# Text context enters with its features on the partitions; keys are multiplied one round sooner

## The reference

```python
# cross attention, 16 heads of 16
q  = layernorm(x) @ Wq + bq
kv = ctx @ Wkv + bkv                      # keys and values of each head
attn = softmax(q . k / 4) over the 77 rows
x1 = x + (attn @ v) @ Wp + bp
# mixture of experts: 8 experts, hidden 1024, the best 2 of each token
xf = layernorm(layernorm(x1)) * g + b
gate = softmax of the two highest of xf @ router_w
expert_e(t) = clip(clip((t_n @ W1 + b1) * silu(clip(t_n @ W2 + b2))) @ Wo + bo)
out = x1 + sum over the two experts of gate_e * expert_e(xf)
```

## Time and profile before

| | before |
|---|---|
| median of 3 runs | 937.87 us |
| lowest, highest | 937.62, 942.07 us |
| span of the profiled execution | 940.2 us (its own run time is not listed apart) |
| instructions | 19225 |
| PE busy | 897.5 us (95%) |
| DVE busy | 745.6 us (79%) |
| ACT busy | 648.5 us (69%) |
| POOL busy | 410.9 us (44%) |
| attention rounds, first scores to first expert product | 19.5 to 309.3 us |

### The profile page before, as it was taken

How to read it: one execution, slowest core, us unless ns; L and a number is a source line. 1 busy time by engine, 2 the same in 40 slices (tenths; PEclk the granted TensorE clock), 3 DMA queues, 4 the chain that set the end, 5 groups by cost and what they waited for, 6 DMA issues and landing times.

```text
span 940.2 us, 19225 instructions
## 1 busy us (share of the span) xinstructions
PE 897.5 (95%) x6206; PEld 806.6 (86%) x6206; DVE 745.6 (79%) x1757; ACT 648.5 (69%) x1305; POOL 410.9 (44%) x649
## 2 busy tenths in 40 slices
PE   5999999999999988999999999999999999999995
PEld 3788887887888877888999989899898998998994
DVE  2678888788688888887988888787877877878893
ACT  3666766767558774776877776776766777767773
POOL 3555576777567577322433150504204233043052
PEclk9999999999799999999999999999999999999998
DMA  5332233342246217744656545736817828566442
GB/s 141 62 66 56 65 87 75 79 99 68 49 111 202 101 65 281 220 121 129 175 135 171 168 119 196 226 119 169 267 66 192 308 54 247 201 163 175 162 79 26
DMA packets 132625, 129.18 MB, mean 137 GB/s; under 512 B 59984, under 2 KB 117408, under 8 KB 132384
## 3 DMA queue, kind: packets, MB, share of 16 engines
q1 hardware_dynamic: 119648, 110.36, 38.5%
q0 software_dynamic: 12864, 17.44, 10.3%
HBM read 102.01 MB, written 25.36 MB: 135 GB/s over the span
## 4 chain that ended last, share of the span: by engine, by line
PE 81%; DVE 7%; issue 4%; ACT 4%; POOL 1%; another core or an unknown queue 1%; SPq 1%; DMA 0%; POOLq 0%; DVEq 0%; ACTq 0%
PE bank L2002 36%; PE bank L2046 19%; PE bank L1835 5%; PE bank L1755 3%; PE bank L1994 3%; PE bank L1812 3%; PE bank L1773 3%; PE bank L1971 2%; PE bank L2034 1%; PE bank L1802 1%; DVE maxes L1256 1%; PE bank L1858 1%; PE bank L1820 1%; DVE probs L1262 1%; PE bank L1868 1%
## 5 line engine op out<-in xcount | busy, mean ns | idle before, releaser
L860 POOL DMA_INDIRECT out_rows<-yo,token x68 | 114.1, 1678 | 379.3 <-ACT yo L1111 314.6
L2002 PE MATMUL bank<-xh,wh 128*128 128x512 f32 (+1 forms) x672 | 234.7, 349 | 2.0 <-DVE gate_in L1628 1.4
L2002 PE MATMUL bank<-xl,wh 128*128 128x512 f32 (+1 forms) x672 | 229.1, 341 | 0.0
L2002 PE MATMUL bank<-xh,wl 128*128 128x512 f32 (+1 forms) x672 | 228.4, 340 | 0.0
L1604 DVE TENSOR_TENSOR wl<-raw,wh 128x1024 fp32r<-128x1024 f32 x126 | 152.6, 1222 | 12.8 <-ACT wh L1042 11.0
L2046 PE MATMUL bank<-wh,hh 128*128 128x256 f32 x496 | 142.1, 286 | 1.1 <-issue 1.0
L2046 PE MATMUL bank<-wl,hh 128*128 128x256 f32 x496 | 140.7, 284 | 1.0 <-issue 1.0
L2002 PEld LDWEIGHTS bank<-xh,wh 128*128 128x128 f32 x672 | 128.3, 191 | 15.5 <-DVE gate_in L1628 2.8
L2046 PE MATMUL bank<-wh,hl 128*128 128x256 f32 x496 | 140.8, 284 | 0.0
L2002 PEld LDWEIGHTS bank<-xh,wl 128*128 128x128 f32 x672 | 128.0, 190 | 14.9
L2002 PEld LDWEIGHTS bank<-xl,wh 128*128 128x128 f32 x672 | 128.4, 191 | 10.9
(11 more groups left out here) (198 smaller groups left out, 1882.0 us busy)
## 6 DMA issues: line engine op xcount, KB each, us to landing
raw<-in_W SPq DMA_DIRECT2D x42, 1024.0 KB
raw<-in_Wo SPq DMA_DIRECT2D x25, 1024.0 KB
whole<-in_W SPq DMA_DIRECT2D x8, 1024.0 KB, 6.6
xs<-in_x SPq DMA_DIRECT2D x32, 128.0 KB, 2.6
out_rows<-x SPq DMA_DIRECT2D x32, 128.0 KB, 1.8
shared<-z_rows SPq DMA_DIRECT2D x7, 520.0 KB
bo_row<-in_bo SPq DMA_DIRECT2D x25, 128.0 KB
k_blocks<-k_parts SPq DMA_DIRECT2D x128, 19.2 KB
```

The costliest lines, as they stand in the source:

```text
L860: e.indirect_dma_start(out=out, out_offset=bass.IndirectOffsetOnAxis(ap=token[j % 4][:, s:s + 1], axis=0), in_=yo[j % 2][:, s, :], in_offs ...
L2002: mm = e.matmul(ps[:, h * cols:(h + 1) * cols], ws[split_before(j) % 2][:, w, c, m * P:(m + 1) * P], xx[j % 2][:, c, 0:cols], start=(h == ...
```

## The change

The host hands the context over as `[8 pairs, 128 features, 2 chunks, 2 batches, 77 rows]`, so one DMA of 128 partitions fills the tile `c_t` that PE reads; there are now two such tiles. `transpose_ctx` on PE and `ctx_t` on ACT are gone. `keys_of_pair`, `keys` and `low_keys` move one round sooner, to the rounds -3, 1, 5, ... 25. SP loads `wk` and `wv` with a counter each, and ahead of `wq`; it stores the values of batch 0 between the first four and the last four pieces of its keys; and it issues the key pieces of odd batches one round sooner, in the rounds -1, 3, 7, .... The turns of the two shared banks shift with the removed use.

```diff
-def ctx_pair(i):
+def key_pair(i):
     return (i + 3) // 4 if (i + 3) % 4 == 0 and 0 <= (i + 3) // 4 < BATCH // 2 else None
...
-        uses += [("k", nb // 2)] if batch and even and nb % 2 == 0 else []
+        uses += [("k", key_pair(i))] if key_pair(i) is not None else []
...
-        uses += [("ctx", ctx_pair(i))] if ctx_pair(i) is not None else []
...
-        cs = [raw[2][0:CTX, 1, i * D:(i + 1) * D] for i in range(2)]
-        c_t, k_t = (raw[2][:, 0, i * 2 * DC * CTX:(i + 1) * 2 * DC * CTX].rearrange(
-            "p (c s k) -> p c s k", c=DC, s=2) for i in range(2))
+        *c_t, k_t = (raw[2][:, 0, i * 2 * DC * CTX:(i + 1) * 2 * DC * CTX].rearrange(
+            "p (c s k) -> p c s k", c=DC, s=2) for i in range(3))
...
-            def load_ctx(b):
-                if b >= 2:
-                    e.wait_ge(ctx_t_mm, b // 2)
-                e.dma_start(cs[b % 2][:, :], a["ctx"][b * CTX:(b + 1) * CTX, :]).then_inc(
-                    f_ctx[b % 2], 16)
+            def load_ctx(t):
+                if t >= 2:
+                    e.wait_ge(v_mm, 2 * (t - 1))
+                e.dma_start(c_t[t % 2][:, :, :, :], a["ctx"][t]).then_inc(f_ctx[t % 2], 16)
...
             load_ctx(0)
             e.dma_start(qk_bias[:, :], a["qk_bias"]).then_inc(f_const, 16)
-            load_ctx(1)
+            load_weights(f_wk, wk, "wk")
             load_x(1)
-            load_weights(f_kv, wk, "wk")
+            load_weights(f_wv, wv, "wv")
             load_weights(f_wq, wq, "wq")
+            load_row(f_bv, 0, "bv")
             load_x(2)
-            load_weights(f_kv, wv, "wv")
-            load_row(f_bv, 0, "bv")
...
                 load_rest(i)
+                if (i + 7) % 4 == 0 and 2 <= (i + 7) // 4 < BATCH // 2:
+                    load_ctx((i + 7) // 4)
                 if batch and i % 2:
                     load_values(nb)
-                    if nb % 2 == 0 and nb + 2 < BATCH:
-                        load_ctx(nb + 2)
-                        load_ctx(nb + 3)
...
                     store_x1(i - 2)
+                if i % 2 and 0 <= nb + 1 < BATCH and (nb + 1) % 2:
+                    spread_keys(nb + 1)
                 if batch and i % 2 == 0:
                     if nb == 0:
-                        spread_keys(nb)
+                        spread_keys(nb, range(HPB))
                     store_values(nb)
-                    if nb:
+                    if nb == 0:
+                        spread_keys(nb, range(HPB, HPC))
+                    elif nb % 2 == 0:
                         spread_keys(nb)
...
-            def ctx_t(t):
-                e.wait_ge(ctx_t_mm, t + 1)
-                if t:
-                    e.wait_ge(v_mm, 2 * t)
-                e.activation(c_t[:, :, :, :].rearrange("p c s k -> p (c s k)"),
-                             misc_of("ctx", t)[:, 0:2 * DC * CTX], ACTF.Copy).then_inc(
-                                 ctx_t_out, 1)
...
-                if batch and even and nb % 2 == 0:
-                    keys(nb // 2)
+                if key_pair(i) is not None:
+                    keys(key_pair(i))
...
+                if key_pair(i) is not None:
+                    low_keys(key_pair(i))
                 if batch and not even:
                     low_queries(nb)
...
-                if 0 < nb < BATCH and even and nb % 2 == 0:
-                    low_keys(nb // 2)
...
-                if batch and even and nb % 2 == 0:
-                    keys_of_pair(nb // 2)
+                if key_pair(i) is not None:
+                    keys_of_pair(key_pair(i))
...
-                if ctx_pair(i) is not None:
-                    transpose_ctx(ctx_pair(i))
```

More of the change, by code:

```diff
@@ L275, in build @@
         v_flat = nc.dram_tensor("v_flat", [BATCH, KEYS, VW], F32, kind="Internal").ap()
-        f_const, f_bv, f_rows, f_kv, f_wq, f_wp, f_router = (
-            sem(n) for n in ("f_const", "f_bv", "f_rows", "f_kv", "f_wq", "f_wp", "f_router"))
+        f_const, f_bv, f_rows, f_wk, f_wv, f_wq, f_wp, f_router = (
+            sem(n) for n in ("f_const", "f_bv", "f_rows", "f_wk", "f_wv", "f_wq", "f_wp",
+                             "f_router"))
         f_x, f_ctx = sems("f_x", XR), sems("f_ctx", 2)
@@ L297, in build @@
                              "recip_made", "attn_made", "best_made", "best_index"))
-        (ctx_t_out, k_out, k_high, xn_t_out, q_out, q_high, exp_made, probs_t_out, attn_t_out,
+        (k_out, k_high, xn_t_out, q_out, q_high, exp_made, probs_t_out, attn_t_out,
          xf_t_out, logits_out) = (
-            sem(n) for n in ("ctx_t_out", "k_out", "k_high", "xn_t_out", "q_out", "q_high",
+            sem(n) for n in ("k_out", "k_high", "xn_t_out", "q_out", "q_high",
                              "exp_made", "probs_t_out", "attn_t_out", "xf_t_out", "logits_out"))
-        (ctx_t_mm, k_mm, v_mm, xn_t_mm, q_mm, scores_mm, probs_t_mm, values_mm, attn_t_mm, proj_mm,
+        (k_mm, v_mm, xn_t_mm, q_mm, scores_mm, probs_t_mm, values_mm, attn_t_mm, proj_mm,
          xf_t_mm, logits_mm, place_mm) = (
-            sem(n) for n in ("ctx_t_mm", "k_mm", "v_mm", "xn_t_mm", "q_mm", "scores_mm",
+            sem(n) for n in ("k_mm", "v_mm", "xn_t_mm", "q_mm", "scores_mm",
                              "probs_t_mm", "values_mm", "attn_t_mm", "proj_mm", "xf_t_mm",
@@ L441, in build @@
         misc, (last_on_bank6, last_on_bank7) = misc_turns()
-        misc_read = {"ctx": lambda b: (ctx_t_out, b + 1), "attn": lambda i: (attn_t_out, i + 1),
+        misc_read = {"attn": lambda i: (attn_t_out, i + 1),
                      "q": lambda b: (q_out, 2 * b + 2), "proj": lambda i: (x1_made, i + 1),
@@ L504, in load_x, with spread_keys @@
                 e.dma_start(xs[i % XR][:, :], a["x"][i * P:(i + 1) * P, :]).then_inc(f_x[i % XR], 16)
-            def load_ctx(b):
-                if b >= 2:
-                    e.wait_ge(ctx_t_mm, b // 2)
-                e.dma_start(cs[b % 2][:, :], a["ctx"][b * CTX:(b + 1) * CTX, :]).then_inc(
-                    f_ctx[b % 2], 16)
+            def load_ctx(t):
+                if t >= 2:
+                    e.wait_ge(v_mm, 2 * (t - 1))
+                e.dma_start(c_t[t % 2][:, :, :, :], a["ctx"][t]).then_inc(f_ctx[t % 2], 16)
             def load_weights(fl, dst, n):
                 e.dma_start(dst[:, :, :], a[n].rearrange("(c p) n -> p c n", p=P)).then_inc(fl, 16)
[L515 to L522, removed]
+            def spread_keys(b, heads=range(HPC)):
+                if heads[0] == 0:
+                    e.wait_ge(k_low, b // 2 + 1)
+                    if b == 0:
+                        e.wait_ge(blocks_ready, 2)
+                    if b >= 2:
+                        e.wait_ge(scores_mm, SCORES_OF_BATCH * (b - 1))
+                for h in heads:
                     part = slice(h * HD, (h + 1) * HD)
@@ L576, in load_rest @@
                     load_x(7)
+                    load_ctx(1)
                 if i == 2:
@@ L1562, in round_ops @@
                     early_slots()
-                if nb == 0 and even:
-                    low_keys(0)
                 if batch and even:
@@ L1775, in transpose_probs @@
                 mm.then_inc(probs_t_mm, 1)
-            def transpose_ctx(t):
-                ps = claim("ctx", t)
-                for s in range(2):
-                    e.wait_ge(f_ctx[s], 16 * (t + 1))
-                    for c in range(DC):
-                        at = (2 * c + s) * CTX
-                        mm = e.transpose(ps[:, at:at + CTX], cs[s][:, c * P:(c + 1) * P],
-                                         ident[0:CTX, 0:CTX])
-                mm.then_inc(ctx_t_mm, 1)
             def transpose_attn(i):
@@ L1852, in keys_of_pair @@
                 ps = claim("k", t)
-                e.wait_ge(ctx_t_out, t + 1)
+                e.wait_ge(f_ctx[t % 2], 16 * (t // 2 + 1))
                 if t == 0:
-                    e.wait_ge(f_kv, 32)
+                    e.wait_ge(f_wk, 16)
                 for m in range(DC):
@@ L1865, in values_of_ctx @@
                 ps = claim("v", b)
-                e.wait_ge(ctx_t_out, b // 2 + 1)
+                e.wait_ge(f_ctx[b // 2 % 2], 16 * (b // 4 + 1))
+                if b == 0:
+                    e.wait_ge(f_wv, 16)
                 for c in range(DC):
-                    mm = e.matmul(ps[0:CTX, 0:D], c_t[:, c, b % 2, :], wv[:, c, :],
+                    mm = e.matmul(ps[0:CTX, 0:D], c_t[b // 2 % 2][:, c, b % 2, :], wv[:, c, :],
                                   start=(c == 0), stop=(c == DC - 1))
@@ L2151 @@
         "x": get("x").reshape(TOKENS, D),
-        "ctx": get("ctx_1024").reshape(BATCH * CTX, D),
+        "ctx": get("ctx_1024").reshape(BATCH // 2, 2, CTX, DC, P).transpose(0, 4, 3, 1, 2),
         "wq": get("L0_xattn_Wq"),
```

3 lines of the change are left out of this document (1 added, 2 removed).

## The result

Four runs of the changed kernel beside four of the one before, on one chip: **949.4 us** (945.1 to 952.89) against 939.5 (937.62 to 942.07), a ratio of 1.0119, 95% interval 1.0072 to 1.0165. It is slower, outside the range of 933.5 to 946.5. The profiled run took 946.71 us with a span of 944.9; the trace of the kernel before has 940.2, and with the same 1.8 us between span and run time it belongs to its longest run, of 942. So the two traces lie 4.7 us apart, where the medians lie 9.9.

A forecast was written before the change was run, and what follows sets the result against it. The prediction took PE to bound the kernel, busy for 95% of the span. Its terms, -2.2 - 2.1 + 5.7 + 0.5 = +1.9 us on a median of 937.9, gave 939.8 us, range 933.5 to 946.5.

The forecast's parts named there:

- SP's queue: Odd batches' key pieces issued a round sooner: behind them only the next `x` load and values store, so no cost.
- the start: Before the first scores: `wk` lands sooner, so key products and pieces start sooner, less one store's issue: -2.2 us.
- the transposes: Seven context transposes of 0.30 us each on PE's path in the rounds go away: -2.1 us.
- the sooner pieces: Odd batches' key pieces one round sooner, so their values load 3 to 6 us sooner: costed at nothing.
- The keys one round sooner: Rounds 9 to 25: key products lose their cover, and five even rounds wait 1.18 us each for DVE: +5.7 us.
- The upper bound: Of the keys' move: five waits of 1.81 us, plus up to 0.49 more per round from `low_keys` before `low_queries`: +11.5.
- The better bound of -3.4: Of the start: if the store costs nothing and PE's start is all that counts, -3.4 us.
- ACT: Odd rounds: ACT's key group ahead of the queries' bias lengthens the projection's wait about 0.1 us five times: +0.5 us.
- A: Rival, even key rounds: DVE catches up as POOL's `v_blocks` move away from `route`; 933 to 935 us, chance 0.25.
- B: Rival, PE's clock: new waits of about 1.8 us bring falls to half rate; 943 to 951 us, chance 0.25.
- C: Rival, the start gives nothing: pieces land no sooner, or the store waits; 942 us, chance 0.1.

The follow-up runs named there:

- kernel 1: Changed kernel with batch 15's key pieces issued in round 28 again, behind the first expert loads: 938.82 us, ratio 1.0073 to the kernel before.
- kernel 5: Changed kernel with the first expert's parameters and first weight matrix issued in round 27, ahead of batch 15's key pieces: 938.91 us, ratio 1.0032.
- kernel 2: Kernel before with only batch 15's key pieces moved to round 27, ahead of the first expert loads: 944.21 us, ratio 1.0107.
- experiment 3: Also called kernel 3: kernel 1 with the keys back in the even rounds from the second pair on: 930.18 us, ratio 0.9964.
- 4: Kernel 3 with 14 unused matmuls as PE's first work: 928.3 us, ratio 0.9927.
- 8: Kernel 5 with the keys back in the even rounds: 930.95 us, ratio 0.9957.
- 10: Kernel 3 with DVE's low part of the keys put back behind `find_slots`: 931.39 us, ratio 0.9946.
- 11: Kernel 3 run once more, unchanged, on another chip: 931.21 us, ratio 0.9934.
- kernel 7: Kernel 3 with the odd batches' key pieces in the rounds they had in the kernel before: 937.24 us, ratio 1.0006.
- 12: Kernel 7 run once more, unchanged, on one chip with 11: 937.57 us, ratio 1.0009.

## Why the prediction was wrong, point by point

**The step that failed** is the one on SP's queue: behind the odd batches' pieces "only the next load of `x` and the next store of values". That holds for the rounds 3 to 23, six times. For batch 15 the pieces moved to round 27, and the next thing on SP is the first expert's load in round 28. I followed the steady cycle and not its last turn. The cost is 9.9 us in the traces; in the medians 4 to 8 (ratios of the changed kernel and of kernels 1 and 5, 0.0046 apart with overlapping intervals, and 0.0087 apart), and 10 for kernel 2. It was in no term, bound or rival. Added to the forecast sum of +1.9 it gives +11.8; the medians measured +9.9. That the two lie so close is luck in part, since two more terms were off, and in opposite directions: the start and the transposes, below, and the sooner pieces.

**The keys one round sooner**, +5.7: right in mechanism and place. The five new waits were 1.36, 0.89, 0.86, 1.53 and 0.86, 1.10 on the mean, where I took 1.18, and pair by pair the keys' rounds cost 5.3 us (experiment 3). In the traces, from the mark of tile 7 to that of tile 27, the last before the stall, the kernels 4, 8, 10 and 11, with the keys in the even rounds, take 177.7 to 178.3 us, kernel 1 184.5 (88.39 to 272.84) and the changed kernel 184.9 (89.33 to 274.23): 6.1 to 7.2 us, of which some is at a lower clock near round 27. Kernel 3 itself takes 180.8, with the low clock of its rounds 17 and 18. The medians have 8.6 (kernels 1 and 3) and 8.0 (5 and 8); the rest goes with the mean granted clock of their runs, 0.985 for kernel 1 and 0.987 for kernel 3, which is not shown to be its cause. The upper bound had DVE's late queries in it, but not that POOL nearly doubles their duration.

**The start**, -2.2: the profile shows 0.9 in the changed kernel and 1.6 in kernel 1 (17.91). `wk` took 3.66 us to land and the products ran from 6.41, not 5.9, so the pieces began at 10.54, not 9.9. The first scores of the other kernels with this start lie between 17.76 and 19.14, 18.5 on the mean, and those of the two traces with the old one at 19.47 and 20.70. The better bound of -3.4 doesn't follow from the terms given: with the store at nothing they make -2.8.

**The transposes**, -2.1, and the start together should show in kernels 7 and 12, which have nothing else of the change that matters: 1.0006 and 1.0009, that is nothing, give or take 3 us. The traces do show the transposes' part: the two rounds with keys (9 and 10, and so on) take 17.72 us in kernel 7 in three of five cycles and 17.82 and 18.69 in the others, where the kernel before and kernel 2 never have less than 18.00. That is the 0.30 us each of the earlier trace rows, and the forecast that it reaches the median was not borne out. The mean granted clock of the runs of kernels 7 and 12 is below that of the kernel before beside them (0.986 and 0.987; 0.985 and 0.988), which may have taken it back; why it is lower is open.

**The sooner pieces**, costed at nothing for all but SP's queue, gained 4 to 6 us in the medians. This second miss went the other way and hid about half of the first; its mechanism is shown only in part.

**ACT**, +0.5: in the five rounds with keys, for which the term was meant, the projection has no wait for ACT's `q_t` at all, and in the rounds 11, 19, 23 and 27 it stayed at 0.17. Nothing was lost there.

**The rivals.** A fell: the even key rounds wait. B was partly right. The fall was there, but behind a stall of 4.6 us of PE, and it came from a cause I had not seen. Its condition, a wait of about 1.8 us, is not what decides: behind the wait of 1.52 in round 22 kernel 5's trace is at 0.52 and 0.50 from 218 to 228 us, while the changed kernel stays at 1.00 behind its 1.53, with PE busy for 2.5 of the 4 us before in both; and kernel 3's has 0.55 to 0.58 from 160 to 168, behind 6 us of which PE was busy for 4.6. C fell in the traces, where the start gained.

Together, by the ratios: transposes and start about 0, sooner pieces -0.4 to -0.75%, keys' round +0.75 to +1.1%, weights behind pieces +0.5 to +0.9% (1.1 in kernel 2). They sum to between +0.5% and +1.6%; measured +1.2%. The kernel with the keys in the even rounds and the weights not behind the pieces (3, 8 and 11) is faster than both: 0.9934 to 0.9964.

## What to carry to other kernels

When a transfer is issued sooner from a queue that works in order, list what stands behind it in every round, the last ones above all, where the next stage's loads begin; a price of nothing in the steady cycle says nothing about its end. Work that fills a wait is free only where it stands: before it is moved, compare the wait that it covers with the one at its new place. And a stall of TensorE costs twice where its clock falls behind it: in these traces 4.4 us of waiting brought 5.5 us of slow clock, which unused matmuls in the idle time took away.

## What the runs showed of the hardware that I had not expected

A DVE subtraction of 128x512 took 0.66 us where it was over before POOL's products began, and 1.22 where POOL was in one of 128x256; POOL's six operations for `v_blocks`, next in line, took 2.22 in place of 1.77. An instruction that is put ahead of another can cost twice its length.

The spread of one kernel's runs goes with the granted clock. Kernel 1's fastest run, 935.13 us, had a mean granted clock of 0.991; its slowest, 949.11, had 0.974. That is 14 us for 0.017, with no change in the program. The stretches at the lower clock stand at other places from trace to trace (234 to 245 us in the kernel before, 160 to 168 in kernel 3, 218 to 228 in kernel 5), and the traces of kernels 7 and 10 have none in the rounds.

After the stall of round 29 the clock stood at 0.50 for 12 us although PE was busy for 11.33 of them; with 74 unused matmuls in the idle time it stayed at 1.00.
